# A fused attention and expert kernel: query and key transposes as rounded products with a unit matrix, and a new order of work

## What is computed

```python
x = x + L0_xattn(layernorm(x), ctx, ctx, mask)   # 16 heads of 8; softmax(q k / sqrt(8)) v, output product
x = x + L0_ffn(layernorm(x))                     # 8 experts of 512, top 2, exact gelu
x = x + L1_xattn(layernorm(x), ctx)              # causal self attention, cross attention, small net, norms
x = x + L1_ffn(layernorm(x))                     # 32 experts of 64, top 6 of 4 groups, and a shared one
```

## Time and profile before

| | us |
|---|---|
| median of 3 runs | 597.49 (597.3 to 597.72) |
| profiled execution, its own time | 596.67 |
| its span, first to last instruction | 594.9 |
| PE busy in the span | 569.7 |
| PEld busy | 374.7 |
| DVE busy | 401.7 |
| ACT busy | 322.5 |
| POOL busy | 105.4 |

### The profile page before, as it was taken

How to read it: one execution, slowest core, us unless ns; L and a number is a source line. 1 busy time by engine, 2 the same in 40 slices (tenths; PEclk the granted TensorE clock), 3 DMA queues, 4 the chain that set the end, 5 groups by cost and what they waited for, 6 DMA issues and landing times.

```text
span 594.9 us, 8098 instructions
## 1 busy us (share of the span) xinstructions
PE 569.7 (96%) x2512; PEld 374.7 (63%) x2512; DVE 401.7 (68%) x1265; ACT 322.5 (54%) x566; POOL 105.4 (18%) x120
## 2 busy tenths in 40 slices
PE   4899999999999999999999899999899999999997
PEld 3556666665566667656676466666666676666664
DVE  6888989774132344666637585777889999768564
ACT  1587688766454476644855348745292542342321
POOL 3111110000111311242202432126201110100000
PEclk9999999999999999999999999999899999999999
DMA  4400000300311100101111011061321233341431
GB/s 119 195 15 10 18 10 2 105 39 19 107 36 35 54 20 19 36 28 54 60 31 44 14 42 44 1 199 39 122 75 51 90 119 98 111 138 62 143 120 56
DMA packets 23306, 38.35 MB, mean 64 GB/s; under 512 B 3776, under 2 KB 9536, under 8 KB 22880
## 3 DMA queue, kind: packets, MB, share of 16 engines
q1 hardware_dynamic: 22832, 37.44, 19.9%
q10 hardware_dynamic: 432, 0.40, 0.2%
HBM read 36.45 MB, written 1.38 MB: 64 GB/s over the span
## 4 chain that ended last, share of the span: by engine, by line
PE 80%; DVE 10%; ACT 4%; issue 2%; POOL 2%; DMA 1%; DVEq 0%; POOLq 0%; ACTq 0%
PE ps L1681 16%; PE ps L1493 9%; PE ps L1495 9%; PE ps L1851 9%; PE ps L1494 9%; PE ps L1488 3%; PE ps L1568 3%; PE ps L1588 3%; PE ps L1500 3%; PE ps L1603 2%; PE ps L1600 2%; PE ps L1758 1%; PE ps L1738 1%; DVE NM L1156 1%; PE ps L1530 1%
## 5 line engine op out<-in xcount | busy, mean ns | idle before, releaser
L1493 PE MATMUL ps<-xThi,w1s 128*128 128x512 f32 x256 | 147.5, 576 | 2.9 <-DVE h L1445 2.6
L911 ACT ACTIVATE h<-ps,early 128x512 f32<-128x512 f32 x128 | 86.7, 687 | 88.8 <-PE ps L1495 68.9
L1681 PE MATMUL ps<-h,w2s 128*128 128x512 f32 x256 | 122.5, 594 | 3.3 <-DVE ty L1245 3.2
L1495 PE MATMUL ps<-xTlo,w1s 128*128 128x512 f32 x256 | 101.4, 396 | 0.0
L1494 PE MATMUL ps<-xThi,w1s 128*128 128x512 f32 x256 | 100.9, 394 | 0.0
L1002 ACT ACTIVATE s<-ps 128x512 f32<-128x512 f32 x68 | 40.7, 598 | 95.4 <-PE ps L1495 93.8
L1493 PEld LDWEIGHTS ps<-xThi,w1s 128*128 128x128 f32 x256 | 48.5, 190 | 37.3 <-issue 18.2
L1681 PEld LDWEIGHTS ps<-h,w2s 128*128 128x128 f32 x256 | 46.2, 189 | 35.5 <-issue 23.8
L1494 PEld LDWEIGHTS ps<-xThi,w1s 128*128 128x128 f32 x256 | 48.7, 190 | 28.6 <-issue 24.3
L776 POOL TENSOR_TENSOR acc_o<-acc_o,ty 128x512 f32<-128x512 f32 x32 | 41.9, 1310 | 140.2 <-DVE ty L1245 115.7
L1445 DVE TENSOR_TENSOR h<-s,ps 128x512 f32<-128x512 f32 x68 | 46.5, 684 | 28.2 <-PE ps L1495 21.0
(11 more groups left out here) (264 smaller groups left out, 889.6 us busy)
## 6 DMA issues: line engine op xcount, KB each, us to landing
CB<-ct_rows SPq DMA_DIRECT2D x128, 128.0 KB, 2.9
WB<-wt_rows SPq DMA_DIRECT2D x32, 256.0 KB, 3.2
w2s<-w_dram SPq DMA_DIRECT2D x2, 2048.0 KB, 8.5
raw<-gu_dram SPq DMA_DIRECT2D x4, 512.0 KB, 3.8
x_in<-x_dram SPq DMA_DIRECT2D x4, 256.0 KB, 2.9
w2s<-dn_dram SPq DMA_DIRECT2D x1, 1024.0 KB, 5.7
out_dram<-ty SPq DMA_DIRECT2D x4, 256.0 KB, 2.9
late<-late_dram SPq DMA_DIRECT2D x1, 608.5 KB, 7.5
```

The costliest lines, as they stand in the source:

```text
L911: nc.scalar.activation(h32[:, c % HR, :], bank[c % 2], ACT.Gelu, bias=b1T[:, c:c + 1]).then_inc(b_gelu.sem, 1)
L1493: M(dst, w[0], xThi[:, x, :], start=start, stop=False)
L1495: return M(dst, w[0], xTlo[:, x, :], start=False, stop=stop)
L1681: M(bank[2], w2s[:, c * P:(c + 1) * P], h32[:, c % HR, :], start=(c % 4 == 0), stop=(c % 4 == 3)).then_inc(b_y.sem, 1)
```

## The change

- A new tile `unit`, 128 x 128 of float32r, is filled on DVE by a cast of `ident`, as a new step of `constants` behind the constant columns of `KN`. It raises `pads`.
- `query_stack` and TensorE's `keys` no longer call the transpose with the tile read as float32 and `ident`: they call the ordinary product `M` with the float32r tile as stationary operand and `unit` as moving one.
- TensorE's first `queries` and the `keys` of batch 0 wait for `pads` at 4.
- All five plans are new. 45 of 128 places in SP's order change, 74 of 116 in POOL's, 287 of 497 in ACT's, and on DVE (942 steps, one more after) and TensorE (914) most do, many by a place or two. At the start DVE's order was `constants`, `normalised` (two steps), `biased`, `normalised` (two), `masks`; it becomes `masks`, `constants`, `normalised` (two), three steps of `constants` with `unit` among them, `normalised`, and `biased` only behind all of `normalised`.

```diff
 PLAN_SP = {
-    "load_x": [[0], [1040], [2704], [5590]],
-    "second_weights": [[14389, 14395, 28061, 38108, 39646, 41268]],
-    "load_context1": [[14407], [24876], [31482], [35078]],
-    "store": [[48439], [50521], [56182], [57613]],
+    "load_x": [[0], [1102], [2647], [4998]],
+    "second_weights": [[16986, 19095, 32632, 36333, 36339, 38256]],
+    "load_context1": [[14333], [24979], [26523], [36345]],
+    "store": [[47810], [49312], [55577], [57007]],
...
 PLAN_DVE = {
-    "constants": [[0, 1037, 1125, 1138, 1211, 1256, 1264, 1272, 16849, 16862]],
-    "normalised": [[581, 672, 844, 863, 882, 906, 925, 976], [1689, 1779, 2102, 2215, 2235, 2357, 2376, 2504], [3660,
-    "masks": [[870, 1030], [1680, 2109], [5054, 5333], [8174, 8462]],
-    "biased": [[720], [2632], [3485], [6714]],
+    "constants": [[450, 720, 729, 743, 851, 1123, 1279, 1287, 1295, 17947, 18055]],
+    "normalised": [[581, 672, 844, 863, 882, 906, 925, 976], [1662, 1753, 1974, 2209, 2254, 2305, 2350, 2439], [3640,
+    "masks": [[443, 897], [1637, 1967], [4852, 5032], [8418, 8437]],
+    "biased": [[1030], [2575], [4602], [6131]],
...
     mhalf = sb("mhalf", [P, NT])
+    unit = sb("unit", [P, P], F32R)
     warm = sb("warm", [P, NT])
...
             V.tensor_copy(KN[:, :, :, 24:26], valid.unsqueeze(2).unsqueeze(3).to_broadcast([P, 2, NH, 2])).then_inc(ones.sem, 1)
             yield
+            V.tensor_copy(unit[:], ident).then_inc(pads.sem, 1)
+            yield
...
         def query_stack(dst, qn, g):
             for i in range(NT):
-                src = qn[:, i, HG * g:HG * g + HG, :].rearrange("p h c -> p (h c)").bitcast(F32)
-                last = nc.tensor.transpose(dst[:, i * P:(i + 1) * P], src, ident)
+                src = qn[:, i, HG * g:HG * g + HG, :].rearrange("p h c -> p (h c)")
+                last = M(dst[:, i * P:(i + 1) * P], src, unit[:], start=True, stop=True)
...
                 pe.wait_ge(a_qn.sem, a_qn.at(b, 3))
+                if b == 0 and g == 0:
+                    pe.wait_ge(pads.sem, NPAD + 1)
                 claim(k)
...
                 if b == 0:
                     pe.wait_ge(ones.sem, 2)
+                    pe.wait_ge(pads.sem, NPAD + 1)
                     pe.wait_ge(zeros.sem, 3)
...
-                    src = KN[:, :, HG * g:HG * g + HG, :].rearrange("p t h c -> p t (h c)").bitcast(F32)
-                    nc.tensor.transpose(dst[:, gg, 0:P], src[:, 0, :], ident)
-                    last = nc.tensor.transpose(dst[:, gg, P:KW], src[0:TP, 1, :], ident[0:TP, 0:TP])
+                    src = KN[:, :, HG * g:HG * g + HG, :].rearrange("p t h c -> p t (h c)")
+                    M(dst[:, gg, 0:P], src[:, 0, :], unit[:], start=True, stop=True)
+                    last = M(dst[:, gg, P:KW], src[0:TP, 1, :], unit[0:TP, 0:TP], start=True, stop=True)
```

More of the change, by code:

```diff
@@ L185 @@
-    "masks": [[870, 1030], [1680, 2109], [5054, 5333], [8174, 8462]],
-    "keys": [[1047, 1092, 1146, 1177, 1223], [2286, 2946, 2979, 3010, 3121], [5347, 5838, 5988, 6019, 6113], [8384,
-        8510, 8829, 8860, 9086]],
-    "values": [[1285, 1626, 1664, 1672, 1767, 1911], [4828, 4874, 5251, 5259, 5287, 5340], [7907, 7952, 8376, 8543,
-        8551, 8705], [10786, 11220, 11257, 11396, 11404, 11412]],
-    "queries": [[1419, 1491, 1553, 1566], [3164, 3345, 3575, 3588], [6253, 6415, 7129, 7238], [9194, 9625, 9687, 9739]
-        ],
@@ new lines @@
+    "values": [[1308, 1353, 1629, 1643, 1651, 2567], [4665, 4858, 5218, 5300, 5308, 5316], [7602, 7781, 8130, 8232,
+        8279, 8287], [10416, 10461, 10512, 10520, 10811, 10819]],
+    "queries": [[1419, 1491, 1553, 1566], [3355, 3427, 3497, 3545], [5995, 6607, 6914, 6927], [8883, 9203, 9265, 9278]
+        ],
+    "biased": [[1030], [2575], [4602], [6131]],
+    "split0": [[4020, 4207, 5690, 5749, 5809, 9140, 9858, 11090]],
+    "maxima": [[1797, 1836, 1890, 1929, 1983, 2021, 2093, 2131, 2182, 2201], [2215, 2266, 2311, 2401, 2490, 2529, 2635,
[9 rows of a table added]
@@ L258 @@
+    "halves_d": [[36712, 36759], [42183, 43858], [46071, 47314], [51068, 52033]],
+    "router": [[35551, 35582, 35614, 35656, 35725, 36110, 36142, 36193, 36314, 36506, 36538, 36570, 36594, 36615],
[3 rows of a table added]
+    "stage_d": [[39392, 39608, 39731, 39795, 39975, 40038, 40128, 40245, 40430, 40547, 40660, 40858, 40986, 41084,
[8 rows of a table added]
 }
 PLAN_PE = {
-    "context_keys": [[720], [1948], [5240], [8257]],
-    "context_values": [[1150], [4648], [7748], [10485]],
-    "inputs": [[1040, 1237], [2576, 3058], [5600, 6147], [8706, 9088]],
@@ L263 @@
-    "queries": [[1653, 2041, 2331, 3664], [4316, 5083, 5976, 6595], [7428, 8100, 8442, 9284], [10043, 11070, 11482,
-        12210]],
-    "keys": [[1408, 1491], [3265, 4499], [6310, 7602], [9405, 10700]],
-    "maxima": [[1792, 1814, 1885, 1923, 1991, 2016, 2085, 2115], [2170, 2208, 2302, 2409, 2478, 2523, 2645, 2659],
[7 rows of a table removed]
-    "scores": [[2247, 2386, 2423, 2500, 2542, 2622], [2827, 3012, 3035, 3216, 3239, 3340], [3617, 3754, 3777, 3860,
[5 rows of a table removed]
-    "values": [[2680, 2885, 3144], [3395, 3518, 3707], [4033, 4185, 4371], [4860, 4984, 5173], [5707, 5831, 6020],
-        [6440, 6639, 6818], [7159, 7283, 7472], [7849, 8001, 8190], [8759, 8917, 9238], [9541, 9725, 9921], [10129,
-        10334, 10579], [10801, 10925, 11114], [11589, 11747, 11979], [12297, 12488, 12684], [12896, 13020, 13199],
-        [13568, 13691, 13871]],
@@ new lines @@
+    "queries": [[1638, 2059, 2105, 3546], [4088, 4860, 5698, 6090], [7112, 7771, 8351, 9045], [9564, 10523, 10552,
+        11555]],
+    "keys": [[1411, 1491], [3719, 3840], [6052, 6768], [8967, 10180]],
+    "maxima": [[1755, 1777, 1848, 1886, 1941, 1979, 2033, 2084], [2168, 2190, 2266, 2317, 2362, 2476, 2572, 2586],
[7 rows of a table added]
+    "scores": [[2221, 2339, 2376, 2445, 2494, 2604], [2794, 2918, 2970, 3093, 3116, 3249], [3509, 3636, 3659, 3754,
[5 rows of a table added]
+    "values": [[2633, 2819, 3153], [3275, 3399, 3578], [3933, 4114, 4293], [4637, 4761, 4960], [5447, 5571, 5750],
+        [6173, 6325, 6534], [6860, 6984, 7301], [7520, 7672, 7871], [8386, 8572, 8883], [9074, 9246, 9443], [9655,
+        9828, 10096], [10272, 10396, 10577], [10997, 11149, 11369], [11810, 11933, 12130], [12394, 12546, 12801],
+        [12951, 13086, 13265]],
@@ new lines @@
+    "output": [[5098, 5298], [8011, 8207], [10716, 10847], [13412, 13629]],
+    "prepare_b": [[11268, 11430, 12251], [14533, 17407, 18664], [20962, 22704, 24107], [27193, 28100, 31648]],
+    "first": [[12701, 13182, 13457, 13715, 13956, 14025, 14235, 14304, 14462, 14620, 14689, 15015, 15084, 15500, 15569,
[8 rows of a table added]
+    "weights": [[13323], [20556], [26015], [33694]],
+    "second": [[13540, 13784, 13870, 14149, 14376, 14757, 14843, 14929, 15156, 15242, 15328, 15414, 15640, 15795,
[8 rows of a table added]
+    "stage_c": [[14105, 14577, 15884, 19555, 19757, 19843], [26430, 26643, 26779, 27104], [33260, 33404, 33852, 33938]
+        , [39447, 40528, 40798, 41638]],
@@ new lines @@
+    "scores_c": [[19929, 20039, 20478, 20780], [26954, 26975, 27460, 27525], [34027, 34164, 34379, 34526], [40973,
+        41132, 41402, 41466]],
+    "turns_c": [[20542, 21339, 21518, 21780], [27614, 27854, 28319, 28491], [34515, 34886, 35169, 35431], [41882,
+        42429, 42523, 42699]],
+    "attends_c": [[20869, 21910, 21953, 22017], [28354, 28376, 28761, 28825], [35477, 35499, 35542, 35606], [42745,
+        42767, 42810, 43029]],
+    "cross": [[22241, 22463, 23163, 23365, 23863, 25454, 25788, 26101], [29238, 29425, 30151, 30263, 30851, 32304,
+        32463, 32861], [35847, 36344, 37035, 37079, 37357, 38288, 38504, 38971], [43253, 43474, 44372, 44415, 44840,
+        46154, 46335, 46782]],
```

180 lines of the change are left out of this document (82 added, 98 removed), and 178 rows, old and new, of tables (PLAN_ACT, PLAN_DVE, PLAN_PE, PLAN_SP).

## The result

The changed kernel takes **599.99 us** (median of 14 runs, 597.8 to 603.33) against 597.50 for the kernel before (14 runs beside it): ratio 1.0047, 95% interval 1.0029 to 1.0064. It is slower by 2.5 us. The profiled execution took 600.07 us, its span 598.3 (before 596.67 and 594.9).

The account below looks back on a forecast made before the run. TensorE was taken as the bound (busy 96%, 80% of the chain). TensorE terms of +1.9 us, counted as +1.5, and start +2.8 on 596.67 gave 601.0; with the median 0.8 above, forecast 601.5 us, range 593.5 to 606.5.

Parts of the forecast that it names:

- The start: DVE's new list queues memsets and statistics behind the late mask; L395 starts at 6.9 us, not 4.03: +2.8 us.
- rival C: At DVE's start, the mask lands with the context or the wait is covered, so no slip: 598.7 us, chance 0.08.
- The slot: Query products at L1500: rounded slot 0.112 us, set by its load, against the transpose's 0.109; 128 products, +0.4 us.
- Rival A: At L1500 rounded products stream in 0.064 us, load hidden or short: 594.9 us, faster; deciding limit 0.087; chance 0.18.
- Rival B: Rounded products with so few columns run like exact ones, 0.222 us, plus 2 us at the keys: 613 us, chance 0.06.
- The share of 80%: TensorE's share of the chain: of +1.9 us added to TensorE, 80% counted as reaching the time, +1.5 us.
- The keys: Key transposes, 8 calls: three exposed loads grow by 0.05, two streams shrink by 0.045; +0.06 each, +0.5 us.
- The exposed loads: Query stacks beginning after a wait: first load in the open, 0.05 us more per stack, 19 stacks, +1.0 us.
- The order otherwise: Reordered entries on five engines, later stages included: long waits may go or others come; 0 +- 5.5 us, taken as 0.
- rival D: New order removes the long waits, 4 us or more: 597.5 or a little below; the other way 606; chance 0.08.

Follow-up runs that it names:

- e4: Kernel before with only the late start put into DVE's list (mask step first, then constants): 600.44 us, ratio 1.0042.
- e3: Changed kernel with the early start given back in DVE's list (constants first, mask step behind the normalisation): 597.67 us, ratio 1.0008.
- e6: e2 with each rounded query product split into two of 64 moving columns: 614.73 us, ratio 1.0290 against the kernel before.
- e7: Kernel before with each query transpose issued twice into the same place: 608.47 us, ratio 1.0182.
- e10: e3 plus two waits holding POOL's wide operations until DVE's four-column normalisation steps finish: 596.30 us, ratio 0.9983 against the kernel before.
- e11: Kernel before plus waits holding POOL's wide operations at its two places until DVE's four-column steps finish: 595.88 us, ratio 0.9979.
- e1: Changed kernel with query and key transposes put back, new order, unit cast and waits kept: 601.88 us, ratio 1.0073 against the kernel before.
- e2: Kernel before, own order, with rounded products exchanged in and the unit cast added on DVE: 597.24 us, ratio 1.0006.
- e13: The same program as e2, timed and profiled a second time: 597.73 us, ratio 1.0009 against the kernel before.
- e8: Kernel before plus three idle exact products of zeros on TensorE at the start: 596.84 us, ratio 0.9985.
- e12: e11 plus the three idle products of e8: 594.63 us, ratio 0.9948 against the kernel before.

## Why the prediction was right, and where it was not

The forecast was 601.5 us, slower; measured were 599.99, inside the range, slower by 2.5 instead of 4.0.

**The start, right in time and in price.** L395 at 6.9 was the forecast, 7.00 the measurement; +2.8 us forecast, +2.8 in e4 and 2.3 in e3. Its two parts hold: the mask does not come earlier (rival C is out), and a late start in front of a stretch led by TensorE is not made good.

**The slot, right.** 0.112 us forecast, 0.107 to 0.112 measured; the cause (the load that shows when nothing long covers it) is what e6 shows. Rival A, 0.064 us, is out: the two halves would have cost nothing more. Rival B, 0.22 us, is out too. Of the two values that the Trainium skill ("TensorE: Matmul & The Clock Gate", sections "Back-to-back issue gap" and "Weight-path perf modes — Fast Weight Load (FWL) and DoubleRow") suggested for the product, about 81 ns and a fast load, neither is seen here: the loads of the rounded product last 192 ns, longer than the transpose's 140.

**The share of 80%, right** for these slots, by e7.

**The keys, mis-sized.** Forecast were +0.06 us a call: three exposed loads longer by 0.05 each and two streams shorter. In TensorE's timeline the call that starts at 44.95 ends at 45.78, where the next product starts: 0.83 us, against 0.82. The first step, from 128 rows to 32, fell from 0.21 to 0.15; the steps from 32 rows to 128 rose from 0.17 to 0.21; the second step from 128 to 32 stayed at 0.26. My step "three exposed loads grow by 0.05" took the load's duration for the gap; the changes of tile size answer differently. It is +0.1 us in 8 calls, not +0.5.

**The exposed loads, mis-sized.** +1.0 us for 19 stacks behind a wait is the largest error among the terms of the sum. Idle time before the line fell from 9.8 us in 21 waits (those of the earlier trace rows, and two of 1.2 us together for ACT) to 8.5 in 16. In the part that holds 92 of the 128 products, exchanging the product costs 0.2 us in one order and 0.4 in the other, and 92 slots longer by 0.003 are 0.3 of that. Nothing in the runs shows the extra 0.05 us a stack on the path. With both terms at nothing the sum is 0.4 + 2.8 = 3.2, less 0.9 to 1.2 for what the order gained: 2.0 to 2.3, against 2.5 measured.

**Missing from the sum: the pace at the start.** The prediction has no term for when TensorE's full pace comes. By the profiles it moved from 21.9 us to 34.2, and batch 0's output product is 5.2 us late where the start alone makes it 2.8. The other 2.4 us do not show in the measured difference: in the profile batches 1 to 3 won back 0.7 us and the later stages 1.1, and the profiled execution of before took 0.8 us less than its median. That the total came within 1.5 us of the forecast is in part luck: two terms were too large, and one was left out whose share in the measured time the runs do not tell apart.

**The order otherwise, near nothing, as taken.** With the same start and product the new order gives 597.67 (e3) and the old one 597.24 and 597.73. It gains about 1 us in the first attention, and nothing of that can be told in the whole time. The waits of the earlier trace rows were not removed (rival D) but replaced by others, and in front of both pairs POOL's wide operations hold DVE's short ones. I had counted those waits as chance of the order. They have a mechanism that could have been read before, at least for the one that shrank in e10 and e11: in the old trace a step on four columns takes 2.34 us beside such a POOL operation. What the product and the order cost may not be a plain sum either, as e1 suggests; its half-clock stretches could hang on small shifts or on the execution, and the runs do not tell which.

**Slips in the working.** The terms add up to 601.0 against the profiled execution and, with the 0.8 us to the median, to 601.8; the forecast says 601.5. Rival A's limit of 0.087 us a slot leaves out the 80%; with it, it is 0.082. Rival B counts 2 us at the keys where the bound given for them is 3.5; with that it comes to 614.7. None of these changes the outcome.

**What stays open.** In the old order the rounded products move the first output product from 57.5 to 59.4 us (e2) and 59.2 (e13), with the full pace coming some 7 us later, and in the new order from 60.4 (e1) to 62.7 (after). The ratios of the timed runs show only 0.4 and 0.5, with 1.4 as the upper end. Part of the gap is in which executions were profiled: that of before took 0.8 us less than the median beside it, that of e13 0.7 more than its own, and that of e2, 600.2, is the slowest of its 12 runs. Whether ordinary rounded products delay the full clock in every execution, and why, the runs do not tell.

## What to carry to other kernels

Price a small TensorE product by the larger of its stream and its load: here, in a rounded product of 128 columns, it is the load, and fewer columns buy nothing. When an order of work is made anew, look at the first entries of each engine's list: one early wait for a late transfer puts everything queued behind it on the path, even clears that used to be free. And read DVE's short dependent steps for durations far above their usual ones: what POOL does beside them is a cost that no wait names, and making POOL wait can move it to the next steps instead of removing it.

## What the runs showed of the hardware

- POOL's wide operations (1.3 to 2.4 us) stretch DVE's operations beside them, from 0.16 to 2.3 us on four columns, and four of 128 columns from 1.1 to 5.3 us in e10. Delaying POOL (e10, e11) moved the stretched durations to the DVE operations that then ran beside it. DVE's operations with one tensor input (L410, L419) are stretched as well as those with two. The Trainium skill, "GPSIMD Engine Reference", section "1. Specifications", says that POOL's interfaces to SBUF are shared with VectorE, and names DVE operations in a two-port mode or with two SBUF inputs; the trace agrees for L404 and L407, and whether L410 and L419 run in such a mode no run here shows.
- TensorE runs at half its pace for most of the first 20 to 34 us, though it is busy for most of that time (e7 and e11 have 3.4 us of full pace from 14.1 and 13.0 us on). Three idle products at the start bring the full pace at 6.6 to 7.7 us. It is lost again from 14 to 17 us on, and the gain is small: 0.5 us in e8, 1.3 in e12 against e11, by the medians.
- The same program can show a stretch of 3.4 us at half the clock behind a wait in one execution and none in the other (e2 and e13 at 425 us, waits of 1.67 and 1.69).
- A rounded product of 128 stationary columns takes a slot of 0.107 to 0.112 us with 128 moving columns and 0.101 to 0.107 with 64 (after, e6).
- At a change between tiles of 128 and of 32 rows a step takes 0.17 to 0.26 us for transposes and 0.15 to 0.26 for rounded products.
